# Turning the rank stacks of a four-stage kernel on VectorE and ScalarE instead of TensorE

## Chip, cores and metric

The program runs on one core of a Trainium2 chip. The metric is the device time of one execution in microseconds, 905.26 us as the median of three runs (903.66 to 906.57).

## What is computed

`x` has 64 batches of 64 tokens with 1024 features. Four stages each add something to it, and the stages' indices choose the weights per batch. Cut to what matters:

```python
def reference(x, lang, cond, ad2, ad3, ...):
    # 0: dense W, plus 8 gated low-rank experts (top 2 of 8, rank 16)
    x = x + (x @ W.T + 2.0 * lora(x, gates(x @ Wr.T, lang), A, B))
    # 1: each batch's own 64x64 matrix mixes its 64 tokens
    x = x + einsum('bct,bcd->bdt', x, weights[cond])
    # 2: adapter of the batch, rank 16:  (x B2^T) A2^T
    x = x + einsum('bnr,bor->bno', einsum('bni,bri->bnr', x, B2[ad2]), A2[ad2])
    # 3: dense W3 and bias, plus adapter of the batch, rank 16
    x = x + x @ W3.T + b3 + 2.0 * einsum('btr,bro->bto', einsum('bti,bir->btr', x, A3[ad3]), B3[ad3])
    return x
```

## The kernel before

All dense work is fp32, done as three matmuls of operands rounded to fp32r (high by high, high by low, low by high). ScalarE makes a high part by a rounding copy, VectorE the low part by a subtraction, each waiting for the one before it by a semaphore.

A first phase (to about 340 us) multiplies the stages' matrices into each other. The second phase, 340 us to the end, works through 32 tiles of 128 tokens (two batches of 64 each), in 16 pairs. The code of every engine is unrolled and written by hand: `fore(j, back, fin)` and the rest of `step(j, ...)` for pairs 0 to 14, `fore` and the rest of `last(j)` for pair 15. In pair j the tiles a = 2j and b = 2j + 1 get their dense product (`plain`, and `winograd` for a Strassen-like half), while the two tiles before, a1 = a - 2 and b1 = a - 1 (b2 = a - 3), are finished. The names on the queues (below, `a1` and so on) are these.

The change concerns how a tile is finished. `mixed` writes the mixed tile and, in its first 64 columns, the hidden values of the two adapters (16 ranks for each of two batches and two adapters) to a PSUM bank. Then:

1. `h2_hi` (ScalarE) and `h2_lo` (VectorE) write the high and low parts of adapter 2's ranks to `h2stack`, 128 tokens x 128 columns, in which the columns of the other batch are zero (set once by GpSimd at the start).
2. `h2_rows` (TensorE, line 1486) turns the 128x128 stack into PSUM, `h2T_copy` (ScalarE) rounds it to `h2T`.
3. `ranks2` (TensorE, lines 1503 and 1465) multiplies `h2T` with the adapter's rows `up2`. Its first matmul corrects adapter 3's hidden values and releases `h3_hi`.
4. `h3_hi`, `h3_lo`, `h3_rows` (line 1491), `h3T_copy` and `ranks3` do the same for adapter 3, after which VectorE adds the bias (`add_bias`) and SyncE stores the tile.

These run twice per pair: for a1 wholly inside `fore`, and for b1 with its adapter 2 at the end of `step` and its adapter 3 at the start of the next pair's `fore`. On the ScalarE queue other work stands between: `ud_hi(b)` writes `u2s` and `d3m` from `mdraw`, the next tile's gathered adapter rows, and so waits for their DMA (`ld_md`). SyncE issues that DMA, `load_md(b)`, after `load_up2(a1)`, which waits for `ranks2(b2)`. `gate_exp(a)` gives VectorE the exponential for its chain `gate(a)` (gden to `hg`), behind which stand `hidden_rows(a)`, `h3_lo(a1)` and the low parts of the next operands. `mix_hi(b1)` waits for GpSimd. TensorE's `repeated(b)` (line 1477) needs `vparts` of `hidden_sum(b)`, on VectorE behind `gate(b)`, behind `hgT_lo(a)`, behind `x0_lo(j + 1)`, which follows ScalarE's `x0_hi(j + 1)`.

Of the kernel before, what the change touches and what calls it, by code (L numbers as in the profile page):

```python
# [16 lines left out]
def build(nc, x, stat, mov, a0, wr, wc, u3, u2k, d3k, bias3, lang_ids, ids, out):  # L17
# [137 lines left out]
    with ctx:  # L155
# [116 lines left out]
        h2stack = sb("h2stack", [P, BT, RANK, 2, 2], F32R)  # L272
        h3stack = sb("h3stack", [P, BT, RANK, 2, 2], F32R)
# [26 lines left out]
        ps_hgT, ps_h2T, ps_h3T = ps_s[:, 0:TOKENS], ps_s[:, TOKENS:2 * TOKENS], ps_s[:, 2 * TOKENS:3 * TOKENS]  # L300
# [10 lines left out]
        def plain_bank(t):  # L311

            return ps_d[0] if (t // 2 + t) % 2 == 0 else ps_d[2]

# [5 lines left out]
        def sem(name):  # L320
# [21 lines left out]
        act_h2, act_h2T, act_h3, act_h3T, act_hgT = map(sem, ("act_h2", "act_h2T", "act_h3", "act_h3T", "act_hgT"))  # L342
# [7 lines left out]
        dve_h2, dve_h3, dve_hgT = map(sem, ("dve_h2", "dve_h3", "dve_hgT"))  # L350
# [6 lines left out]
        pe_group, pe_hl, pe_ud, pe_rep, pe_h, pe_mix, pe_h2T, pe_h3, pe_up2, pe_hgT, pe_h3T = map(  # L357
            sem, ("pe_group", "pe_hl", "pe_ud", "pe_rep", "pe_h", "pe_mix", "pe_h2T", "pe_h3", "pe_up2", "pe_hgT", "pe_h3T"))
# [3 lines left out]
        CONSTS = 6  # L362
        SETS = BT + 8
# [14 lines left out]
        def _(sp):  # L378
# [189 lines left out]
            sp.wait_ge(pool_const, CONSTS)  # L568
# [68 lines left out]
        def _(pool):  # L637
# [7 lines left out]
            nc.gpsimd.memset(h2stack[:, :, :, :, :].rearrange("p b r h e -> p (b r h e)").bitcast(F32), 0.0).then_inc(pool_const, 1)  # L645
            nc.gpsimd.memset(h3stack[:, :, :, :, :].rearrange("p b r h e -> p (b r h e)").bitcast(F32), 0.0).then_inc(pool_const, 1)
# [124 lines left out]
        def _(act):  # L771
# [120 lines left out]
            def h2_hi(t):  # L892
                act.wait_ge(pe_h, t + 1)
                for b in range(BT):
                    rows = slice(b * TB, (b + 1) * TB)
                    last = round_to(h2stack[rows, b, :, :, 0], hidden(t, rows, slice(b * RANK, (b + 1) * RANK)))
                last.then_inc(act_h2, 1)

            def h3_hi(t):
                act.wait_ge(pe_h3, t + 1)  # L900
                for b in range(BT):
                    rows = slice(b * TB, (b + 1) * TB)
                    last = nc.scalar.activation(h3stack[rows, b, :, :, 0], hidden(t, rows, slice(BR + b * RANK, BR + (b + 1) * RANK)),
                                                ACT.Copy, scale=SCALE3)
# [59 lines left out]
            def fore(j, back, fin):  # L964
# [10 lines left out]
                if back:  # L975
                    h2_hi(a1)
                gate_exp(a)
                ud_hi(b)
                after_P1(j)
                if back:  # L980
                    h2T_copy(a1)
# [4 lines left out]
            def step(j, back, fin):  # L986
# [10 lines left out]
                if back:  # L997
                    h2_hi(b1)
                ud_hi(a + 2)
# [3 lines left out]
                if back:  # L1003
                    h2T_copy(b1)
# [35 lines left out]
        def _(dve):  # L1040
# [88 lines left out]
            nc.vector.tensor_scalar(rbias[:, :, :], rbias[:, :, :], LANG_BIAS, None, ALU.mult).then_inc(dve_set, 1)  # L1129

# [8 lines left out]
            dve.wait_ge(dve_set, BT + 7)  # L1139
# [72 lines left out]
            def stack_lo(t, rows, b, cols, stacked, scale):  # L1212

                src = out_bank(t, 0)[rows, cols][:, :, None].to_broadcast([TB, RANK, 2])
                return nc.vector.scalar_tensor_tensor(out=stacked[rows, b, :, :, 1], in0=src, scalar=scale,
                                                      in1=stacked[rows, b, :, :, 0].bitcast(F32), op0=ALU.mult,
                                                      op1=ALU.subtract)

# [542 lines left out]
```

## Time and profile before

| | |
|---|---|
| median of three runs | 905.26 us (903.66 to 906.57) |
| profiled execution, its own time | 906.27 us |
| its span | 904.5 us |
| TensorE busy, matmul / weight load | 895.8 us / 795.4 us |
| VectorE, ScalarE, GpSimd busy | 557.5, 345.8, 234.9 us |
| granted TensorE clock | 1.00 throughout |
| two stack transposes on TensorE | 32 of each, mean 271 and 279 ns |
| ScalarE's copies to h2T and h3T | 32 of each, mean 274 and 277 ns |

Durations of matmuls overlap, since they are pipelined; what one costs TensorE is read from start to start. A wait in the profile is put down to what ended it. The profiled time lies 1.8 us above its span, which is what lies around the span, and 1.0 us above the median.

### The profile page before, as it was taken

The page shows a single profiled execution, that of the slowest core. Times are in us where ns is not written, and L with a number is a line of the kernel's source. Part 1 is how long each engine was busy: PE and PEld are TensorE (multiplying, and loading weights), DVE is VectorE, ACT ScalarE, POOL GpSimd, SP SyncE. Part 2 cuts the span into 40 slices and gives each one's busy share as a digit, 9 for nine tenths or more (in the row PEclk, how much of TensorE's full clock was granted, in tenths as well). Part 3 has the DMA queues.
Part 4 walks back from the last instruction along what each step waited for, and adds up shares of the span by engine and source line. Part 5 has one row for each costly group of instructions (what it writes and reads, how often), then busy time and mean ns, then how long its engine had stood idle before and what let it go on. Part 6 is the DMA issues. An engine that isn't in the chain of part 4 may idle for free.

```text
span 904.5 us, 14862 instructions
## 1 busy us (share of the span) xinstructions
PE 895.8 (99%) x4758; PEld 795.4 (88%) x4758; DVE 557.5 (62%) x1421; ACT 345.8 (38%) x800; POOL 234.9 (26%) x379
## 2 busy tenths in 40 slices
PE   9999999999999999999999999999999999999997
PEld 7888888888888888998998998998998999989997
DVE  6655444354357526567667677677676676676675
ACT  5543343333334333333434433434424334334333
POOL 1000010011010003523424433424415325324240
PEclk9999999999999999999999999999999999999999
DMA  7978686999663564666766766766666567666664
GB/s 248 309 252 287 208 252 202 311 338 270 186 190 119 172 211 132 189 179 185 218 181 189 216 188 182 210 194 192 190 197 213 168 189 226 182 174 216 184 199 155
DMA packets 105602, 187.69 MB, mean 208 GB/s; under 512 B 15926, under 2 KB 66870, under 8 KB 105526
## 3 DMA queue, kind: packets, MB, share of 16 engines
q1 hardware_dynamic: 105526, 186.76, 67.7%
q8 instruction: 38, 0.62, 0.3%
q14 instruction: 38, 0.31, 0.1%
HBM read 143.20 MB, written 49.81 MB: 213 GB/s over the span
## 4 chain that ended last, share of the span: by engine, by line
PE 92%; DMA 3%; SPq 2%; issue 1%; POOL 1%; DVE 0%; ACT 0%; DVEq 0%; POOLq 0%
PE ps_o L1407 28%; PE ps_d L1433 17%; PE ps_w L1441 13%; PE ps_d L1441 10%; PE ps_s L1407 9%; PE ps_o L1454 5%; PE ps_d L1448 4%; PE ps_o L1465 2%; DMA mdraw<-t 2%; PE ps_s L1471 1%; SPq L445 1%; PE ps_w L1448 1%; DMA chunk_a_raw<-mov 1%; SPq L473 1%; PE ps_o L1503 1%
## 5 line engine op out<-in xcount | busy, mean ns | idle before, releaser
L1042 DVE TENSOR_TENSOR stat_lo<-stat_raw,stat_hi 128x1024 fp32r<-128x1024 f32 (+1 forms) x127 | 146.3, 1152 | 25.8 <-ACT stat_hi L773 23.5
L773 ACT ACTIVATE stat_hi<-stat_raw 128x1024 fp32r<-128x1024 f32 (+1 forms) x127 | 116.8, 933 | 20.5 <-POOL stat_raw L657 6.3
L1433 PE MATMUL ps_d<-w_hi,stat_hi 128*128 128x512 f32 x256 | 105.0, 410 | 0.0
L1433 PE MATMUL ps_d<-w_lo,stat_hi 128*128 128x512 f32 x256 | 101.1, 395 | 0.0
L1433 PE MATMUL ps_d<-w_hi,stat_lo 128*128 128x512 f32 x256 | 100.8, 394 | 0.0
L1407 PE MATMUL ps_o<-chunk_a_hi,stat_hi 128*128 128x512 f32 x216 | 84.4, 391 | 0.6 <-DVE chunk_a_lo L1042 0.6
L1407 PE MATMUL ps_o<-chunk_a_lo,stat_hi 128*128 128x512 f32 x216 | 84.1, 389 | 0.0
L1407 PE MATMUL ps_o<-chunk_a_hi,stat_lo 128*128 128x512 f32 x216 | 84.0, 389 | 0.0
L682 POOL CAST w_hi<-mdraw 128x512 fp32r<-128x512 f32 x32 | 19.6, 614 | 208.8 <-DMA mdraw<-t 208.8
L657 POOL TENSOR_TENSOR stat_raw<-stat_raw,ident 128x128 f32<-128x128 f32 x40 | 21.8, 546 | 186.3 <-DMA stat_raw<-stat 186.3
L1407 PE MATMUL ps_o<-chunk_b_hi,stat_hi 128*128 128x512 f32 x152 | 59.1, 389 | 0.0
L1407 PE MATMUL ps_o<-chunk_b_hi,stat_lo 128*128 128x512 f32 x152 | 59.1, 389 | 0.0
L1407 PE MATMUL ps_o<-chunk_b_lo,stat_hi 128*128 128x512 f32 x152 | 59.1, 389 | 0.0
L1433 PEld LDWEIGHTS ps_d<-w_lo,stat_hi 128*128 128x128 f32 x256 | 48.1, 188 | 11.4
L1433 PEld LDWEIGHTS ps_d<-w_hi,stat_hi 128*128 128x128 f32 x256 | 48.5, 189 | 9.8 <-DVE udb L1246 0.3
L1433 PEld LDWEIGHTS ps_d<-w_hi,stat_lo 128*128 128x128 f32 x256 | 48.4, 189 | 8.1
L1259 DVE TENSOR_TENSOR outb<-ps_o,bias_row 128x356 f32<-128x356 f32 (+1 forms) x93 | 42.0, 507 | 13.1 <-PE ps_o L1465 12.6
L1407 PEld LDWEIGHTS ps_o<-chunk_a_hi,stat_hi 128*128 128x128 f32 x216 | 40.5, 188 | 9.9 <-DVE chunk_a_lo L1042 1.3
L773 ACT ACTIVATE y_hi<-y_raw 128x356 fp32r<-128x356 f32 x48 | 24.0, 499 | 64.8 <-DVE y_raw L1288 48.8
L1407 PEld LDWEIGHTS ps_o<-chunk_a_lo,stat_hi 128*128 128x128 f32 x216 | 40.6, 188 | 8.5
L1407 PEld LDWEIGHTS ps_o<-chunk_a_hi,stat_lo 128*128 128x128 f32 x216 | 40.6, 188 | 8.2
L718 POOL TENSOR_TENSOR stat_raw<-stat_raw 128x512 f32<-128x512 f32 x32 | 45.3, 1415 | 5.5 <-DMA stat_raw<-x 4.0
(226 smaller groups left out, 2269.7 us busy)
## 6 DMA issues: line engine op xcount, KB each, us to landing
up<-tu SPq DMA_DIRECT2D x124, 256.0 KB, 4.4
stat_raw<-stat SPq DMA_DIRECT2D x59, 512.0 KB, 4.2
mdraw<-t SPq DMA_DIRECT2D x128, 208.0 KB, 2.9
stat_raw<-x SPq DMA_DIRECT2D x32, 512.0 KB, 3.5
out<-outb SPq DMA_DIRECT2D x30, 512.0 KB, 5.4
t<-md_a SPq DMA_DIRECT2D x16, 576.0 KB, 5.8
rows_raw<-x SPq DMA_DIRECT2D x32, 256.0 KB, 3.5
chunk_a_raw<-mov SPq DMA_DIRECT2D x24, 256.0 KB, 5.2
```

The source lines that it names most:

```text
L657: nc.gpsimd.tensor_tensor(out=raw[:, s, :], in0=raw[:, s, :], in1=ident[:, :], op=ALU.add).then_inc(pool_stat, 1)
L682: last = nc.gpsimd.tensor_copy(w[part][:, :, MD_AT:P_AT].rearrange("p k (q r) -> p k q r", r=RANK), rows.rearrange("p q (k r) -> p k q r", ...
L718: nc.gpsimd.tensor_tensor(out=dst, in0=in0, in1=in1, op=op).then_inc(pool_s, 1)
L773: return nc.scalar.activation(dst, src, ACT.Copy)
L1042: return nc.vector.tensor_tensor(out=dst, in0=src, in1=rounded.bitcast(F32), op=ALU.subtract)
L1259: nc.vector.tensor_tensor(out=dst[:, OX[n]], in0=out_bank(turn, n)[:, OK[n]], in1=bias_row[:, OX[n]], op=ALU.add).then_inc(dve_out[n], 1)
L1407: last = nc.tensor.matmul(ps_g[g % BANKS][:, :], st[g % RING][a][:, k, :], mchunk[c % 2][v][:, k, :], start=k == 0 and m == 0, stop=k == K ...
L1433: last = nc.tensor.matmul(plain_bank(t)[:, 0:WCOLS], rows[a][:, k, :], w[c][:, k, :], start=k == 0 and m == 0, stop=k == KB - 1 and m == l ...
L1441: last = nc.tensor.matmul(ps[:, 0:SH], rows[a][:, k, :], weights[c][:, k, :], start=first and k == 0 and m == 0, stop=k == HALF_KB - 1 and ...
L1448: last = nc.tensor.matmul(ps, hgT[t % 2][a][:, :], b03[c][:, cols], start=first and m == 0, stop=m == len(PASSES) - 1, skip_group_check=True)
L1454: last = nc.tensor.matmul(out_bank(turn, n)[:, 0:OW[n]], mix[turn % 2][a][:, :], y[t % 2][c][:, Y[n]], start=first and m == 0, stop=m == l ...
L1465: return nc.tensor.matmul(out_bank(turn, n)[:, OK[n]], stackT[:, :], up[:, OX[n]], start=first, stop=True, skip_group_check=True)
```

## The change

The other batch's columns are no longer kept as zeros in the stack: `h2stack` and `h3stack` are 128 x 64. VectorE turns the whole stack by one operation (`turn_ranks`), which turns each 32x32 square in its place, into one buffer `turned` that all places share. ScalarE then rounds the eight squares to their places in `h2T` or `h3T` by eight operations (`place_squares`); the rest of `h2T` and `h3T` is zeroed once on VectorE. Semaphore `dve_turned` counts the turns and `act_turned` the placings, in one order for both adapters (`h2_place`, `h3_place`), so that a turn waits for the placing before it. `place_squares` also waits until TensorE has read the stack before (`pe_up2` and `pe_h3`, or `pe_out[2]`). `ranks3(b2)` is issued one block of `plain(a)` later (after six blocks, not five), `ranks3(a1)` at the same place but without a transpose halfway. On ScalarE `h2T_copy(a1)` now stands before `gate_exp(a)`, and `h2T_copy(b1)` before `ud_hi(a + 2)`.

```diff
-        h2stack = sb("h2stack", [P, BT, RANK, 2, 2], F32R)
-        h3stack = sb("h3stack", [P, BT, RANK, 2, 2], F32R)
+        h2stack = sb("h2stack", [P, RANK, 2, 2], F32R)
+        h3stack = sb("h3stack", [P, RANK, 2, 2], F32R)
+        turned = sb("turned", [P, 4 * RANK])
...
+        def h2_place(turn):
+            return 2 * turn + (0 if at(turn, TURN_A) else 1)
+        def h3_place(turn):
+            return 2 * turn + (3 if at(turn, TURN_B) else 2)
...
+            def place_squares(rows):
+                for b in range(BT):
+                    for i in range(b * TB, (b + 1) * TB, SQUARE):
+                        for q in range(0, 4 * RANK, SQUARE):
+                            row = b * 4 * RANK + q
+                            last = round_to(rows[row:row + SQUARE, i:i + SQUARE], turned[i:i + SQUARE, q:q + SQUARE])
+                last.then_inc(act_turned, 1)
...
             def h2T_copy(t):
-                act.wait_ge(pe_h2T, t + 1)
-                round_to(h2T[:, :], ps_h2T).then_inc(act_h2T, 1)
+                act.wait_ge(dve_turned, h2_place(t))
+                if not at(t, 0):
+                    act.wait_ge(pe_up2, t)
+                    act.wait_ge(pe_h3, t)
+                place_squares(h2T)
 
             def h3T_copy(t):
-                act.wait_ge(pe_h3T, t + 1)
-                round_to(h3T[:, :], ps_h3T).then_inc(act_h3T, 1)
+                act.wait_ge(dve_turned, h3_place(t))
+                if not at(t, 0):
+                    act.wait_ge(pe_out[2], t)
+                place_squares(h3T)
...
+            def turn_ranks(stacked, place):
+                if place > 1:
+                    dve.wait_ge(act_turned, place - 1)
+                nc.vector.transpose(turned[:, :], stacked[:, :, :, :].rearrange("p r h e -> p (r h e)").bitcast(F32)
+                                    ).then_inc(dve_turned, 1)
...
             def ranks2(t):
-                pe.wait_ge(act_h2T, t + 1)
+                pe.wait_ge(act_turned, h2_place(t))
...
-                plain(a, range(0, 3))
-                if fin:
-                    h3_rows(b2)
-                plain(a, range(3, 5))
+                plain(a, range(0, 6))
                 if fin:
                     ranks3(b2)
-                plain(a, range(5, KB)).then_inc(pe_hl, 1)
+                plain(a, range(6, KB)).then_inc(pe_hl, 1)
...
-                plain(b, range(0, HALF_KB))
+                plain(b, range(KB)).then_inc(pe_hl, 1)
+                if back:
+                    ranks3(a1)
                 pe.wait_ge(dve_udb, a + 1)
-                if back:
-                    h3_rows(a1)
-                plain(b, range(HALF_KB, KB)).then_inc(pe_hl, 1)
-                if back:
-                    ranks3(a1)
                 gated_rows(a)
```

Where instructions move, the queues read as follows. On ScalarE, in `fore` of a pair in the middle, from the high part of the ranks of a1 to its last placing (`part` is the copy of a product out of PSUM), before:

```order
L773 ACTIVATE h2stack<-ps_o 64x32 x2
L887 ACTIVATE gexp<-gdiff 128x1
L773 ACTIVATE u2s<-mdraw 128x2x8x16
L773 ACTIVATE d3m<-mdraw 128x2x8x16
L773 ACTIVATE part<-ps_w 128x356
L773 ACTIVATE h2T<-ps_s 128x128
L773 ACTIVATE mix_hi<-mix_raw 128x128
L903 ACTIVATE h3stack<-ps_o 64x32 x2
L773 ACTIVATE h3T<-ps_s 128x128
```

and now, over the same stretch:

```order
L782 ACTIVATE h2stack<-ps_o 64x32 x2
L782 ACTIVATE u2s<-mdraw 128x2x8x16
L782 ACTIVATE d3m<-mdraw 128x2x8x16
L782 ACTIVATE h2T<-turned 32x32 x8
L896 ACTIVATE gexp<-gdiff 128x1
L782 ACTIVATE part<-ps_w 128x356
L782 ACTIVATE mix_hi<-mix_raw 128x128
L916 ACTIVATE h3stack<-ps_o 64x32 x2
L782 ACTIVATE h3T<-turned 32x32 x8
```

`u2s`, `d3m` (`ud_hi(b)`, behind the DMA of `mdraw`) now come straight after the ranks, then the eight squares to `h2T`, and only then the exponential; the copy out of `part` comes after both.

On VectorE, the end of the program, from the first stack of tile 31 (TURN_A, whose rows come after those of tile 30, TURN_B) to the bias of tile 30 (`y_lo<-ps_w` is `Lb_lo`), before:

```order
L1215 SCALAR_TENSOR_TENSOR h2stack<-ps_o,h2stack 64x32 x2
L1042 TENSOR_TENSOR y_lo<-y_raw,y_hi 128x356
L1215 SCALAR_TENSOR_TENSOR h3stack<-ps_d,h3stack 64x32 x2
L1042 TENSOR_TENSOR y_lo<-ps_w,y_hi 128x356
L1215 SCALAR_TENSOR_TENSOR h3stack<-ps_o,h3stack 64x32 x2
L1259 TENSOR_TENSOR stat_raw<-ps_d,bias_row 128x312
```

and now:

```order
L1244 SCALAR_TENSOR_TENSOR h2stack<-ps_o,h2stack 64x32 x2
L1252 STREAM_TRANSPOSE turned<-h2stack 128x64
L1069 TENSOR_TENSOR y_lo<-y_raw,y_hi 128x356
L1244 SCALAR_TENSOR_TENSOR h3stack<-ps_d,h3stack 64x32 x2
L1252 STREAM_TRANSPOSE turned<-h3stack 128x64
L1069 TENSOR_TENSOR y_lo<-ps_w,y_hi 128x356
L1244 SCALAR_TENSOR_TENSOR h3stack<-ps_o,h3stack 64x32 x2
L1252 STREAM_TRANSPOSE turned<-h3stack 128x64
L1299 TENSOR_TENSOR stat_raw<-ps_d,bias_row 128x312
```

Each stack is followed by its turn, and since a turn waits for the placing before it, the subtraction behind it on VectorE waits too.

## Rows read from the trace of the kernel before

**Rows 1.** Page, busy time of each engine over the span.
```profile
PE 895.8 (99%) x4758; PEld 795.4 (88%) x4758; DVE 557.5 (62%) x1421; ACT 345.8 (38%) x800; POOL 234.9 (26%) x379
```

**Rows 2.** Waits over the whole span: us in total, times, longest.
```profile
ACT u2s L773 <- DMA mdraw<-t: 46.8, 28, 3.5
...
PEld ps_s L1491 <- issue: 5.2, 10, 1.1
...
PE ps_s L1491 <- DVE h3stack L1215: 1.4, 3, 0.7
```

**Rows 3.** PE timeline, pair 7: start us, duration us, instruction.
```profile
588.64 0.33 PE L1441 MATMUL ps_w<-B_lo,stat_hi 128*128 128x356 f32 x1
588.80 0.27 PE L1486 MATMUL ps_s<-ident,h2stack 128*128 128x128 f32 x1
588.83 0.41 PE L1441 MATMUL ps_d<-B_hi,stat_hi 128*128 128x356 f32 x1
589.08 0.33 PE L1441 MATMUL ps_d<-B_hi,stat_lo 128*128 128x356 f32 x1
...
590.88 0.32 PE L1503 MATMUL ps_o<-up,h2T 128*128 128x344 f32 x1
...
594.04 0.40 PE L1433 MATMUL ps_d<-w_lo,stat_hi 128*128 128x512 f32 x1
594.53 0.30 PE L1491 MATMUL ps_s<-ident,h3stack 128*128 128x128 f32 x1
...
597.47 0.64 PE L1465 MATMUL ps_o<-up,h3T 128*128 128x312 f32 x3
```

**Rows 4.** Tile ps_s, transposes of h2stack: count, ns min/median/max, first and last start.
```profile
L1486 PE MATMUL ps_s<-ident,h2stack x32: 270/270/274, 379.5 to 894.9; 128*128 128x128 f32 x32
```

**Rows 5.** ACT timeline of the same pair.
```profile
586.07 0.40 ACT L773 ACTIVATE h2stack<-ps_o 64x32 fp32r<-64x32 f32 x2 [0.78 <-PE ps_o L1454]
...
588.81 0.42 ACT L773 ACTIVATE u2s<-mdraw 128x256 fp32r<-128x256 f32 x1 [0.33 <-DMA mdraw<-t]
589.14 0.40 ACT L773 ACTIVATE d3m<-mdraw 128x256 fp32r<-128x256 f32 x1
...
593.36 0.31 ACT L773 ACTIVATE mix_hi<-mix_raw 128x128 fp32r<-128x128 f32 x1 [3.17 <-POOL mix_raw L706]
593.58 0.38 ACT L903 ACTIVATE h3stack<-ps_o 64x32 fp32r<-64x32 f32 x2
```

**Rows 6.** ACT groups by shape: busy us, mean ns, idle before.
```profile
L773 ACT ACTIVATE stat_hi<-stat_raw 128x1024 fp32r<-128x1024 f32 x91 | 96.0, 1055 | 10.7 <-DMA stat_raw<-x 5.3 <-POOL stat_raw L657 5.3
...
L773 ACT ACTIVATE y_hi<-y_raw 128x356 fp32r<-128x356 f32 x48 | 24.0, 499 | 64.8 <-DVE y_raw L1288 48.8 <-DVE y_raw L1273 15.9
...
L773 ACT ACTIVATE h2stack<-ps_o 64x32 fp32r<-64x32 f32 x62 | 12.0, 193 | 15.4 <-PE ps_o L1454 15.0
...
L773 ACT ACTIVATE mix_hi<-mix_raw 128x128 fp32r<-128x128 f32 x32 | 9.9, 310 | 63.5 <-POOL mix_raw L706 63.5
```

**Rows 7.** ACT and PE timeline, the two pairs with the widest and narrowest margin.
```profile
658.58 0.40 ACT L773 ACTIVATE d3m<-mdraw 128x256 fp32r<-128x256 f32 x1
...
660.65 0.32 PE L1503 MATMUL ps_o<-up,h2T 128*128 128x344 f32 x1
...
834.94 0.40 ACT L773 ACTIVATE d3m<-mdraw 128x256 fp32r<-128x256 f32 x1
...
836.05 0.43 PE L1503 MATMUL ps_o<-up,h2T 128*128 128x344 f32 x1
```

**Rows 8.** DVE and PE timeline, pair 7: last vparts and its reader.
```profile
602.45 0.18 DVE L1239 TENSOR_TENSOR vparts<-vsum,vparts 64x32 fp32r<-64x32 f32 x1
...
603.49 0.18 PE L1477 MATMUL ps_s<-vparts,repeat 128*128 128x32 f32 x1
```

**Rows 9.** ACT and PE timeline, end of the program.
```profile
898.88 0.28 ACT L773 ACTIVATE h3T<-ps_s 128x128 fp32r<-128x128 f32 x1 [1.22 <-PE ps_s L1491]
...
899.21 0.73 PE L1465 MATMUL ps_o<-up,h3T 128*128 128x312 f32 x3
```

More of the change, by code:

```diff
@@ L893, in h2_hi @@
                 act.wait_ge(pe_h, t + 1)
+                if not at(t, 0):
+                    act.wait_ge(dve_turned, h2_place(t - 1))
                 for b in range(BT):
                     rows = slice(b * TB, (b + 1) * TB)
-                    last = round_to(h2stack[rows, b, :, :, 0], hidden(t, rows, slice(b * RANK, (b + 1) * RANK)))
+                    last = round_to(h2stack[rows, :, :, 0], hidden(t, rows, slice(b * RANK, (b + 1) * RANK)))
                 last.then_inc(act_h2, 1)
@@ L976, in fore @@
                     h2_hi(a1)
+                ud_hi(b)
+                if back:
+                    h2T_copy(a1)
                 gate_exp(a)
-                ud_hi(b)
                 after_P1(j)
                 if back:
-                    h2T_copy(a1)
                     mix_hi(b1)
@@ L998, in step @@
                     h2_hi(b1)
+                    h2T_copy(b1)
                 ud_hi(a + 2)
@@ L1129, in _ @@
             nc.vector.tensor_scalar(rbias[:, :, :], rbias[:, :, :], LANG_BIAS, None, ALU.mult).then_inc(dve_set, 1)
+            for rows in (h2T, h3T):
+                nc.vector.tensor_copy(rows[:, :], mixraw[:, :]).then_inc(dve_set, 1)
             for first in (0, 2 * BR):
@@ L1221, in h2_lo @@
                 for b in range(BT):
-                    last = stack_lo(t, slice(b * TB, (b + 1) * TB), b, slice(b * RANK, (b + 1) * RANK), h2stack, 1.0)
+                    last = stack_lo(t, slice(b * TB, (b + 1) * TB), slice(b * RANK, (b + 1) * RANK), h2stack, 1.0)
                 last.then_inc(dve_h2, 1)
+                dve.wait_ge(dve_h2, t + 1)
+                turn_ranks(h2stack, h2_place(t))
             def h3_lo(t):
@@ L1227, in h3_lo @@
                 for b in range(BT):
[L1228 removed]
+                    last = stack_lo(t, slice(b * TB, (b + 1) * TB), slice(BR + b * RANK, BR + (b + 1) * RANK), h3stack, SCALE3)
                 last.then_inc(dve_h3, 1)
+                dve.wait_ge(dve_h3, t + 1)
+                turn_ranks(h3stack, h3_place(t))
             def hidden_sum(t):
@@ L1482, in gated_rows @@
                 nc.tensor.transpose(ps_hgT, hg[:, :, :].rearrange("p e r -> p (e r)"), ident[:, :]).then_inc(pe_hgT, 1)
-            def h2_rows(t):
-                pe.wait_ge(dve_h2, t + 1)
-                nc.tensor.transpose(ps_h2T, h2stack[:, :, :, :, :].rearrange("p b r h e -> p (b r h e)").bitcast(F32),
-                                    ident[:, :]).then_inc(pe_h2T, 1)
-            def h3_rows(t):
-                pe.wait_ge(dve_h3, t + 1)
-                nc.tensor.transpose(ps_h3T, h3stack[:, :, :, :, :].rearrange("p b r h e -> p (b r h e)").bitcast(F32),
-                                    ident[:, :]).then_inc(pe_h3T, 1)
             def hidden_ranks(turn, t):
```

61 lines of the change are left out of this document (24 added, 37 removed).

## Prediction, made before the changed kernel ran

> **What bounds the kernel now.** I began with the page: TensorE is busy 895.8 of 904.5 us, ScalarE only 38%, VectorE 62% [rows 1]. The view of the waits says the same from the other side: TensorE waits for nobody in the second phase but in front of the transpose of `h3stack`, 1.4 us for VectorE and 5.2 us of its weight loads without a named releaser [rows 2]. So every slot taken off TensorE is worth its length, and every wait put on it costs its length; what the other engines spend counts only through such waits. The timeline of one pair in the middle (pair 7, about 34.8 us, as the 13 from 2 to 14 are) then shows how far ahead of TensorE the other queues are where the change touches them.
>
> **What is removed.** A transpose is shown as 270 ns [rows 4], but that is its latency. From start to start: 588.64 to 588.80 is 0.16 for a product of 356 columns; with the transpose between, 588.80 to 589.08 is 0.28 [rows 3]. So a transpose takes 0.115 of TensorE, and 64 of them 7.4 us, 55 in pairs 1 to 14 (6.3 us), 9 in the last. The waits before `h3_rows(a1)` go too: 594.04 to 594.53 is 0.49 where a 512-column product is else followed after 0.24 (twelve and the transpose fill 594.53 to 597.47) [rows 3]. Weights are loaded about a slot ahead, so of the 6.6 us of these waits [rows 2] in 13 places I take 13 x 0.25 as covered and 3.2 us as lost. Together 9.5 us saved in pairs 1 to 14.
>
> **What is added: the price of a placing.** Eight ScalarE operations of 32x32 from SBUF. From SBUF, 128 columns take 310 ns and 356 take 499 [rows 6], 0.83 ns a column, so 32 take 230. How closely do they follow one another? `u2s` takes 0.42 and `d3m` starts 0.33 after it; `mix_hi` takes 0.31 and `h3stack` starts 0.22 after it [rows 5]: an overlap of 0.09. But the two operations of `h2stack`, of 193 ns [rows 6], take 0.40 together [rows 5], no overlap. Length isn't what differs, I think, but place: that pair goes from partitions 0 to 63 to partitions 64 to 127, while the overlapping ones start at the same partition. In `place_squares` each square goes to another group of partitions than the one before, so I take 0.24 apiece, 1.91 for eight. The bound from below is the overlap, 0.14 apiece, 1.2 for eight. The Trainium skill (VectorE: DVE Perf Modes, section on two Vector instructions with no wait between them) has a rule for this: an instruction whose start quadrant differs from that of the last access is held until all before it have finished. It states it for VectorE; rows 5 look as if ScalarE does the same. The same page (section on the TRN2 errata) warns that many small tiles pay the fixed latency each time, which speaks against eight squares in place of one copy.
>
> The turn on VectorE, 128x64 from SBUF, has no row. The nearest are a 64x32 operation, 0.18 [rows 8], and ScalarE's 128x128 copy at 0.31; I take 0.25, with 0.15 and 0.6 as ends. It sits in chains with slack, except in (c) and (d).
>
> **(b) ranks2(a1).** Its operand now comes last out of: DMA of `mdraw`, `u2s`, `d3m`, eight squares. In pair 7 `d3m` ends at 589.54 (589.14 + 0.40), held by the DMA [rows 5], as in 28 cases of `ud_hi` [rows 2], and before, one copy followed and `ranks2` started at 590.88 [rows 3], a margin of 1.34. The DMA's issue hangs on `ranks2(b2)` through SyncE's queue, so it doesn't move relative to TensorE. Now the squares end 1.91 - 0.09 after `d3m`, and 0.05 later TensorE goes: 1.87. TensorE itself arrives 0.23 earlier, two transposes being gone. The wait is 2.10 less the margin: 0.76 here. The margin was read in all 13 pairs 2 to 14: from 0.71 (834.94 + 0.40 to 836.05) to 1.67 (658.58 + 0.40 to 660.65) [rows 7], mean 1.08. That makes 13 x 1.02 = 13.2 us, and the first pair, whose landing is late too, 1.3 more: **14.5 us of new waits**.
>
> **(c) Behind it.** The exponential comes after the squares, so VectorE's gate chain starts up to 3 us later. Counting through the queues of pair 7 from the start R of `ranks2(a1)`, with the chain of `gate(b)` as the model for an undisturbed gate: exponential at R, `hg` at R + 1.8, `udb` R + 3.1, `h3_lo` done R + 3.6, turned R + 4.0, placed R + 6.0; TensorE reaches `ranks3(a1)` at R + 6.17 (597.47 - 590.88 less the 0.42 of transpose and wait [rows 3]). Just in time. Then `x0_hi` (1.05 for 1024 columns [rows 6]) and `x0_lo` (about 1.2) end at R + 8.3, 0.5 later than before, and with them all up to `vparts(b)`, which was ready at 602.63 for a reader at 603.49 [rows 8], but with TensorE 0.42 later than it now is: it lacks 0.1. I take 0.13 x 14 = 1.8 us. `ranks3(b2)` gets its stack 1.3 later, is itself 0.6 later (a block more, a transpose less) and had 0.9 in hand: no wait. `h2T_copy(b1)` runs where ScalarE otherwise waits for the DMA of `mdraw` [rows 2]: nothing. The start loses two memsets on GpSimd and gains two copies on VectorE under the first phase's products: nothing.
>
> **(d) The last pair.** Here the chains lie behind one another and TensorE has little else. By the same prices, with the one buffer `turned` in series, TensorE's lag behind its old times is 0.3 us at `ranks3(a1)`, 0.8 at `ranks2(b1)`, 1.8 at `ranks3(b1)`, 2.3 at tile 30's `ranks2`, 2.6 at tile 31's, 3.3 at tile 30's `ranks3`, 5.8 at tile 31's. The last step is the largest: before, a copy of 0.28 at 898.88 let the last matmuls start at 899.21 [rows 9]; now the stack of tile 31 is written after the squares of tile 30 and `Lb`, then turned, then placed by 1.9 us. The bias of tile 30 is out of the way by then (0.3): **+5.5 us**, the nine transposes counted.
>
> **The sum.** -9.5 + 14.5 + 1.8 + 5.5 = +12.3 us. The profiled execution took 906.27 us (its span and 1.8 around it) and would take 918.6; the median of the runs lies 1.0 lower, so 917.6, and I say 918. With placings of 1.8 to 2.0 us, and the small waits of (c) between none and double, 910 to 925.
>
> **Rivals.**
> 1. *The squares overlap* (placing 1.2 us). Then the waits of (b) are 1.40 less the margin, 5.0 us with the first pair, those of (c) vanish, the last pair costs about 2: -9.5 + 5.0 + 2 = -2.5, **902.8 us**. For it speak the overlaps of rows 5, against it the pair of `h2stack` there. It decides below about 0.16 us per square. By the Trainium skill (ScalarE: Activation LUTs, section What ACT_TABLE_LOAD costs) an ACTIVATE with immediate scale takes 186 ns + 0.833 ns a column and back-to-back ones overlap by about 93 ns; by that, eight would take 1.05 us and the time would be about 901, an estimate from that page. Chance 0.22.
> 2. *The turn is slow or is hindered by GpSimd* (0.6 us instead of 0.25). It stands three times in each pair's tight chains: `ranks3(a1)` then waits 0.2 and (c) 0.35 more, 14 x 0.45 = 6 us, and 1.5 in the last pair: **925 us**. For it speaks only that no row shows such an operation; against it, that every row of VectorE with up to 64 columns lies near 0.2. Chance 0.10.
> 3. *The waits and savings cancel*, if the squares take about 0.18 each or the `mdraw` rows land a microsecond sooner, since the DMA is less crowded when TensorE stands: -9.5 + 9 + 1 = about 0, **906 us**. Chance 0.06.
>
> The forecast has 0.62. 0.3% is 2.7 us, about what a measurement of this kernel can tell from no change. Rival 1 lies about that bound and goes mostly to faster: faster 0.18, same 0.09, slower 0.73. The range reaches to rival 1 and rival 2: 901 to 925.
>
> **What would show it.** Right: TensorE's waits name ScalarE's `h2T` in front of `ranks2` in nearly all 14 pairs, some 1 us each, and `h2T` groups of eight last 1.9 us; ScalarE's busy time grows by about 100 us; the gate's `gden` waits for `gexp` in every pair; the last matmuls start 5 to 6 us later relative to the last pair's start. Wrong: squares that start 0.14 apart; TensorE without waits at `ranks2`, with a span about 5 us below mine for each 0.03 us a square is cheaper; or waits in front of `ranks3(a1)`, which would mean a slow turn.

## The result, and the profile after

The changed kernel takes 932.0 us (median of six runs, 926.1 to 941.9); the kernel before, on the same chip, 905.2 us. The ratio is 1.029, interval 1.025 to 1.033 (it leaves out the slowest run, 941.9, which lies over 1.5% above the fastest): 27 us slower, where the forecast was 13. The profiled execution took 926.12 us, 19.9 more than the one before; its span is 924.2 us, its mean granted clock 0.995. The other runs have clocks from 0.995 down to 0.986, and their times rise as the clock falls. Before, it was 1.00.

The page, busy time of each engine:

```profile
PE 900.4 (97%) x4694; PEld 792.2 (86%) x4694; DVE 549.3 (59%) x1487; ACT 444.0 (48%) x1248; POOL 234.8 (25%) x377
```

Against [rows 1], ScalarE has 98 us more. TensorE has 64 instructions fewer and is busy 4.6 us longer, which is the first oddity. The squares, from the page's costliest groups (busy us, mean ns, idle before):

```profile
L782 ACT ACTIVATE h3T<-turned 32x32 fp32r<-32x32 f32 x256 | 57.9, 226 | 30.7 <-DVE turned L1252 28.1
...
L782 ACT ACTIVATE h2T<-turned 32x32 fp32r<-32x32 f32 x256 | 57.9, 226 | 13.0 <-DVE turned L1252 10.3
```

The waits over the span (us in total, times, longest), to be held against [rows 2]:

```profile
DVE gden L1205 <- ACT gexp L896: 42.8, 17, 4.5
...
ACT u2s L782 <- DMA mdraw<-t: 41.3, 17, 4.1
...
PEld ps_o L1533 <- ACT h2T L782: 16.0, 15, 2.5
...
PE ps_o L1533 <- ACT h2T L782: 11.6, 14, 2.2
...
PE ps_o L1505 <- ACT h3T L782: 3.0, 2, 1.7
...
PEld ps_s L1522 <- DVE udb L1286: 2.4, 11, 0.2
...
PEld ps_s L1517 <- DVE vparts L1279: 1.7, 8, 0.3
```

L1533 is the first product of `ranks2`: the forecast's wait stands there, in 14 of 15 pairs. Something stands there that wasn't forecast. The timeline of pair 6, the one with the longest wait (start us, duration us):

```profile
554.88 0.89 SPq L468 DMA_DIRECT2D mdraw<-t  x2
...
562.41 0.42 ACT L782 ACTIVATE u2s<-mdraw 128x256 fp32r<-128x256 f32 x1 [4.09 <-DMA mdraw<-t]
...
563.04 1.88 ACT L782 ACTIVATE h2T<-turned 32x32 fp32r<-32x32 f32 x8
...
564.97 0.19 PEld L1533 LDWEIGHTS ps_o<-up,h2T 128*128 128x128 f32 x1 [2.52 <-ACT h2T L782]
564.98 0.43 PE L1533 MATMUL ps_o<-up,h2T 128*128 128x344 f32 x1 [2.23 <-ACT h2T L782]
...
565.92 0.40 PE L1473 MATMUL ps_d<-w_hi,stat_lo 128*128 128x512 f32 x1
...
566.15 0.40 PE L1473 MATMUL ps_d<-w_lo,stat_hi 128*128 128x512 f32 x1
...
567.16 0.63 PE L1473 MATMUL ps_d<-w_lo,stat_hi 128*128 128x512 f32 x1
...
567.58 0.63 PE L1473 MATMUL ps_d<-w_hi,stat_hi 128*128 128x512 f32 x1
```

The rows land 7.5 us after their issue (554.88, and `u2s` starts at 562.41), where it is 5.5 to 6.3 in the 14 pairs of the kernel before; two roundings and eight squares follow; TensorE stands from 562.75 (the end of its last product) to 564.98. Then, from about 566.5, the same products of 512 columns start 0.42 us apart and not 0.23. The stretches of that time (PE, PEld, DVE, ACT and POOL busy, granted clock, DMA share, GB/s) say why:

```profile
563.00:565.00 2.00, 0.02 (x1) 0.03 (x1) 0.00 (x0) 1.89 (x10) 2.00 (x5) 1.00 0.65 157
565.00:566.00 1.00, 1.00 (x6) 0.95 (x7) 0.64 (x4) 0.97 (x5) 0.63 (x2) 1.00 0.57 229
566.00:567.00 1.00, 1.00 (x5) 0.80 (x4) 0.90 (x5) 0.12 (x1) 0.01 (x1) 0.75 0.04 16
567.00:568.00 1.00, 1.00 (x3) 0.73 (x3) 0.96 (x4) 0.00 (x0) 0.00 (x0) 0.50 0.70 246
568.00:569.00 1.00, 1.00 (x4) 0.80 (x3) 0.95 (x5) 0.23 (x2) 0.00 (x0) 0.50 0.87 238
569.00:570.00 1.00, 1.00 (x4) 0.81 (x3) 1.00 (x3) 0.95 (x5) 0.00 (x0) 0.55 0.16 41
570.00:571.00 1.00, 1.00 (x6) 0.79 (x6) 0.70 (x2) 0.95 (x4) 0.00 (x0) 1.00 0.00 0
```

TensorE ran at 0.50 of its clock, the lower of its levels (1.2 GHz), for 3.4 us, 1.5 us after it had gone to work again. The same follows the wait of pair 1, the second longest (2.0 us in this view), and no other in this profile before the end of the program. Each period costs 1.7 us (half of 3.4), and since a slow product counts as busy, TensorE's busy time grows.

Further small waits sit around the gate's transpose. From pair 11's timeline:

```profile
757.55 0.25 DVE L1286 SCALAR_TENSOR_TENSOR udb<-ps_s,is_lo,vsign 128x32 fp32r<-128x32 f32 x1
757.60 0.33 PE L1481 MATMUL ps_d<-T_lo,stat_hi 128*128 128x356 f32 x1
757.85 0.14 PEld L1522 LDWEIGHTS ps_s<-ident,hg 128*128 128x128 f32 x1 [0.22 <-DVE udb L1286]
757.86 0.33 PE L1522 MATMUL ps_s<-ident,hg 128*128 128x128 f32 x1
758.17 0.41 PE L1494 MATMUL ps_o<-y_hi,mix_hi 128*128 128x376 f32 x1
```

The transpose comes 0.1 late (0.26 after the product ahead of it, where 0.16 is normal), and the product behind it starts 0.31 after it; in the kernel before that step is 0.05 on average. A wait of 0.1 costs 0.3.

The end, of tile 31's stack:

```profile
917.12 0.24 DVE L1252 STREAM_TRANSPOSE turned<-h3stack 128x64 f32<-128x64 f32 x1
...
917.40 1.90 ACT L782 ACTIVATE h3T<-turned 32x32 fp32r<-32x32 f32 x8 [0.89 <-DVE turned L1252]
...
919.35 0.74 PE L1505 MATMUL ps_o<-up,h3T 128*128 128x312 f32 x3 [1.75 <-ACT h3T L782]
```

It answers to [rows 9]. From `ranks2` of pair 15 to these last matmuls it takes 28.4 us before and 33.5 now: 5.1 more.

**Where the time is.** Profiled run against profiled run, +19.7 us of span: +1.9 up to pair 1's `ranks2`, +12.5 from there to pair 14's, +0.6 to pair 15's, +5.1 in the last part, -0.4 behind it. I took every start-to-start step of TensorE from the records and compared them kind by kind. A wait is from here on such a step less the usual 0.16, so it is 0.16 longer than in the views (pair 6: 2.39 for 2.23). For pairs 1 to 14 this gives: waits at `ranks2(a1)` +12.6 (13.2 now, 0.43 to 2.39 in 13 pairs and none in pair 7; the kernel before waited 0.6 in pair 1), the products that restart behind them +1.2, two periods at half clock +3.4, the steps at `repeated` and `gated_rows` +4.7, one wait of 1.5 at `ranks3(b2)` in pair 7, transposes and their waits -9.4. Together +14.0. Up to pair 14's `ranks2` 14.4 is there, and of that 0.5 is lost in the first phase already, by 122 us.

### The profile page after: what moved, and what is told of

Same layout as the page of the kernel before. It is cut to its first block, busy times and chain, and to the rows that moved or that the text cites. A ratio compares the mean times of both kernels' runs of the same rounds, so it can differ in the third digit from the quotient of the medians.

```text
span 924.2 us, 15418 instructions
## 1 busy us (share of the span) xinstructions
PE 900.4 (97%) x4694; PEld 792.2 (86%) x4694; DVE 549.3 (59%) x1487; ACT 444.0 (48%) x1248; POOL 234.8 (25%) x377
## 4 chain that ended last, share of the span: by engine, by line
PE 74%; SPq 8%; DMA 8%; ACT 4%; issue 4%; DVE 2%; POOL 0%; DVEq 0%; ACTq 0%; POOLq 0%
PE ps_o L1447 26%; PE ps_d L1473 11%; PE ps_w L1481 10%; PE ps_s L1447 9%; DMA mdraw<-t 7%; PE ps_d L1481 6%; PE ps_d L1488 4%; SPq L455 3%; PE ps_o L1494 3%; ACT h2T L782 3%; SPq L483 2%; PE ps_o L1505 2%; SPq L468 2%; PE ps_o L1533 1%; SPq L470 1%
## 5 line engine op out<-in xcount | busy, mean ns | idle before, releaser
L1069 DVE TENSOR_TENSOR stat_lo<-stat_raw,stat_hi 128x1024 fp32r<-128x1024 f32 (+1 forms) x127 | 137.0, 1079 | 38.5 <-ACT stat_hi L782 36.2
L691 POOL CAST w_hi<-mdraw 128x512 fp32r<-128x512 f32 x32 | 19.7, 615 | 208.6 <-DMA mdraw<-t 208.6
L782 ACT ACTIVATE h3T<-turned 32x32 fp32r<-32x32 f32 x256 | 57.9, 226 | 30.7 <-DVE turned L1252 28.1
L782 ACT ACTIVATE h2T<-turned 32x32 fp32r<-32x32 f32 x256 | 57.9, 226 | 13.0 <-DVE turned L1252 10.3
```

The lines of the kernel that those rows point to most:

```text
L691: last = nc.gpsimd.tensor_copy(w[part][:, :, MD_AT:P_AT].rearrange("p k (q r) -> p k q r", r=RANK), rows.rearrange("p q (k r) -> p k q r", ...
L782: return nc.scalar.activation(dst, src, ACT.Copy)
L1069: return nc.vector.tensor_tensor(out=dst, in0=src, in1=rounded.bitcast(F32), op=ALU.subtract)
```

## Experiments

Theory: TensorE's waits at `ranks2(a1)` hang on the landing of the `mdraw` rows and on the squares behind it; the longest of them cost a second time, through the clock. Rivals: the squares cost wherever they stand; the clock falls for another reason; the gate that comes late is the main loss. All ratios are to runs of the kernel before on the same chip, whose medians were 905.4 to 906.0 us.

**The earlier rows, e2.**

```
-                if back:
-                    load_up2(a1)
                 if not at(j, 0):
                     choose(b)
                     load_md(b)
+                if back:
+                    load_up2(a1)
```

(and likewise in the last pair)

> SyncE issues the load of the second tile's rows ahead of the load of the first tile's rank rows, in every pair; nothing else differs from the changed kernel. Theory A (the wait at the first rank products is set by the landing of these rows, 5.3 to 7.6 us after their issue, since the rounding of them stands ahead of the squares on ScalarE): the landing moves 1 to 2 us earlier, the waits shrink by as much, from 13.6 us to some 2 us over 14 pairs, no half clock is seen, and the time is 912 to 917 us. Rival B (the issue waits for a buffer that comes free no earlier, or the transfers share the same queues so that the landing stays): the waits stay as they are, 926 to 932 us. Rival C: the rank rows now land too late for the same products: a wait of TensorE for that load, 930 us or more.

907.8 us (ratio 1.0023, 1.0008 to 1.0038): 24 of the 27 us are gone, by an exchange of two loads in a queue. Timeline of pair 9:

```profile
650.13 0.88 SPq L468 DMA_DIRECT2D mdraw<-t  x2
...
656.03 0.42 ACT L782 ACTIVATE u2s<-mdraw 128x256 fp32r<-128x256 f32 x1 [0.36 <-DMA mdraw<-t]
...
656.66 1.89 ACT L782 ACTIVATE h2T<-turned 32x32 fp32r<-32x32 f32 x8
...
658.57 0.20 ACT L896 ACTIVATE gexp<-gdiff 128x1 f32<-128x1 f32 x1
...
659.93 0.32 PE L1533 MATMUL ps_o<-up,h2T 128*128 128x344 f32 x1
```

The squares last 1.89 us as they did, but end 1.4 us ahead of the product. No wait at `ranks2` is left over 0.15 us in pairs 1 to 14, and no half clock before the end (0.998). Theory A: the landing was what `ranks2` waited for. The time is 4 us under the range that I gave. Between the profiled spans lie 17.8 us and between the medians 24.2, so part of this gain is in what the slower runs of the changed kernel have above the profiled one.

**The squares first, e1.** ScalarE's list: squares, exponential, `ud_hi`, where the change has `ud_hi`, squares, exponential.

> ScalarE's list in the first half of a pair is put in another order: the squares of the first tile stand ahead of the exponential of the gate and ahead of the u2s rounding, so that they no longer wait for the rows that a transfer brings. Theory A (the changed kernel's time comes from TensorE's waits at the first rank products, of 0.43 to 2.39 us a pair and 13.6 us over 14 pairs, and from the half-clock periods behind the two longest of them, 3.4 us in the profiled run): these waits and both periods go, and so does what follows on them. The removed transposes' gain of 9.4 us stays, and the last pair keeps its 4.7 us: some 901 us, with the clock at 1.00 up to the last pair. Rival B (the squares themselves slow the kernel wherever they stand, since ScalarE then does everything behind them 1.9 us later: the u2s rounding and with it the hidden product, the gate): the wait moves to another product, 915 us or more. Rival C (the clock falls for another reason than the waits): half-clock periods stay in the trace though the waits are gone.

914.3 us (1.011, 1.008 to 1.014). The waits at `ranks2` and the half clock went; the 901 did not come. The rows are still late here, and now `ud_hi` stands behind them and the squares, so `vparts` and `udb` are late in their turn: in the waits, `ps_s` L1517 for `vparts` has 3.5 us in 11 places and L1522 for `udb` 3.0 in 13, and the steps there add up to 7.4 us more than before over 13 pairs. My expectation left out what stands behind the squares; Rival B has a part in it.

**The gate first, e3 and e7.** The exponential and `ud_hi` ahead of the squares, once with the late rows and once with the early ones.

```
-                ud_hi(b)
-                if back:
-                    h2T_copy(a1)
                 gate_exp(a)
+                ud_hi(b)
+                if back:
+                    h2T_copy(a1)
```

> Only the exponential of the gate and the u2s rounding change places with the squares in the first half of a pair: exponential, rounding, squares. The wait for the rows stays ahead of the squares, so the waits at the first rank products stay (13.6 us) and the half-clock periods with them. What can move is the other part: in the changed kernel the exponential stands behind the squares, some 4.5 us later against the rest than before, and VectorE's chain behind it makes the gate's transpose and the products next to it late, 0.1 to 0.3 us at three places, 4.7 us over 14 pairs. Theory A: these 4.7 us go, 926 to 928 us. Rival B: they hang on the h3 rows' late squares and not on the gate: no change, 932 us.

> Both orders together: SyncE issues the load of the second tile's rows ahead of the rank rows (which took the first rank products' wait away, 907.8 us), and ScalarE takes the gate's exponential and the u2s rounding ahead of the squares (which took the small waits around the gate's transpose away, 4 us over 14 pairs). Theory A: the two costs are apart and add: no wait at the first rank products, none around the gate, the removed transposes' 9.4 us stay, the last pair costs its 4.7 us: 901 to 904 us, no slower than the kernel before. Rival B (the exponential ahead pushes the squares 0.6 us later, past the margin that the earlier rows gave): part of the waits comes back, 906 to 910 us.

e3: 922.0 us (918.7 to 928.2; 1.020, 1.014 to 1.025). The steps around the gate are back at those of the kernel before (their sum is 0.6 us under it, from 4.7 above), while the waits at `ranks2` (17.0 us, 3.8 more than in the changed kernel) and two half-clock periods stayed. So the gate's place was worth its 4.7 us. The median is 10 us lower, and 4 us under what Theory A said, where the profiled spans differ by 3.7; no trace shows the rest. But e7 took 915.4 us, 7.6 worse than e2. Its timeline, pair 10:

```profile
696.90 0.61 POOL L691 CAST w_hi<-mdraw 128x512 fp32r<-128x512 f32 x1 [1.59 <-DMA mdraw<-t]
...
698.73 0.20 ACT L896 ACTIVATE gexp<-gdiff 128x1 f32<-128x1 f32 x1 [2.13 <-DVE gdiff L1199]
...
699.46 1.89 ACT L782 ACTIVATE h2T<-turned 32x32 fp32r<-32x32 f32 x8
...
701.39 0.42 PE L1533 MATMUL ps_o<-up,h2T 128*128 128x344 f32 x1 [0.36 <-ACT h2T L782]
```

The rows are there at 696.9, but ScalarE stands for 2.1 us at the exponential, which waits for VectorE, with the squares queued behind it. `ranks2` waits in every pair again, 0.46 us at least. The two gains are not independent, as I had assumed. It is Rival B's mechanism, and 5 us more than the most that Rival B gave: the exponential's own wait for VectorE was in neither sum.

**The price of a square, e4, e9 and e10.** e4:

```
-                for b in range(BT):
-                    for i in range(b * TB, (b + 1) * TB, SQUARE):
-                        for q in range(0, 4 * RANK, SQUARE):
-                            row = b * 4 * RANK + q
-                            last = round_to(rows[row:row + SQUARE, i:i + SQUARE], turned[i:i + SQUARE, q:q + SQUARE])
+                for q in range(0, 4 * RANK, SQUARE):
+                    for i in range(0, TOKENS, SQUARE):
+                        last = round_to(rows[q:q + SQUARE, i:i + SQUARE], turned[q:q + SQUARE, q:q + SQUARE])
```

> The same sixteen squares a tile and the same 32 x 32 elements each, but read from and written to the same partitions: four from partitions 0 to 31 into partitions 0 to 31, then four from 32 to 63 into 32 to 63. The rank products multiply something else by it; nothing else differs. Theory A (two roundings on ScalarE overlap by 0.09 us only while the range of partitions stays the same, as my prediction took it): six of the seven steps in a group shrink from 0.240 to 0.15 us, a group lasts 1.35 us and not 1.89, each first rank product starts 0.5 us earlier, and with fewer half-clock periods the time is 918 to 924 us. Rival B (the step of 0.24 us is that of a square of 32 columns and 32 partitions, whatever it touches): a group lasts 1.89 us and the time is the changed kernel's, 926 to 934 us.

Its timeline, and the time 908.0 us (1.0029, 1.0008 to 1.005):

```profile
399.79 0.25 DVE L1250 STREAM_TRANSPOSE turned<-h2stack 128x64 f32<-128x64 f32 x1
400.07 1.19 ACT L782 ACTIVATE h2T<-turned 32x32 fp32r<-32x32 f32 x8 [0.74 <-DVE turned L1250]
```

The products multiply something else by this edit, so the run tells of time alone. A group lasts 1.19 us and not 1.89. Inside it squares start 0.120 us apart, 0.224 at the one step that changes partitions; each takes 0.213, so they overlap by 0.093. The first `ranks2` waits fall from 13.2 to 6.8 us, the half clock is gone from the profiled run, the steps around the gate are 1.4 us above those before and not 4.7, and the last part takes 30.1 us. Theory A, and by 10 us more than I had it. The ten runs fall into two groups: six of 903.9 to 908.7 us with clocks of 0.998 and 0.999, four of 910.6 to 912.1 with 0.994 to 0.996, so longer waits and half clock still come in some. By the Trainium skill (ScalarE: Activation LUTs, section What ACT_TABLE_LOAD costs) back-to-back ones overlap by about 93 ns: the trace agrees where the partitions stay, and shows none of it where they change.

e9 asks which of the two ranges counts: squares with the same destination stand one behind the other, their sources differ.

```
-                    for i in range(b * TB, (b + 1) * TB, SQUARE):
-                        for q in range(0, 4 * RANK, SQUARE):
+                    for q in range(0, 4 * RANK, SQUARE):
+                        for i in range(b * TB, (b + 1) * TB, SQUARE)[::1 if q == 0 else -1]:
```

> The changed kernel with its eight squares in another sequence and nothing else: the two that go to the same partitions stand one behind the other (the source's partitions change between them), so that four of the seven steps in a group keep the destination's partitions. The run with all squares in place had steps of 0.120 us where both ranges stayed and 0.224 us where both changed. Theory A (it is the destination's range that decides): a group lasts 0.22 + 4 x 0.12 + 3 x 0.24 = 1.4 us and not 1.89, the first rank products' waits shrink by 0.5 us each, and the time is 914 to 922 us. Rival B (a change of either range keeps two roundings apart): all steps stay at 0.24 us, 926 to 934 us.

931.3 us, all steps 0.237 to 0.241, the group 1.90: Rival B. In the change's own sequence it is the destination that changes at every step, and the source at three of seven; here the source changes at five and the destination at three. Either keeps two squares apart. That the partitions have to be the same, and not the elements (in e4 four squares read the same source), `u2s` and `d3m` show, which differ in their elements alone and overlap by 0.09 [rows 5]. With the early rows the new sequence does nothing either:

> The new sequence of the squares together with the earlier load of the second tile's rows. If the sequence shortens a group to 1.4 us, what was left in the version with the earlier rows, small waits around the gate's transpose of some 0.4 us a pair, shrinks too, and the last pair has 8 groups that are 0.45 us shorter, three or four of them on its path: 903 to 906 us. If the sequence changes nothing: 907.8 us again.

907.9 us (1.0027, 1.0016 to 1.0038).

**The clock, e5 and e6.** e5 puts six idle products of 356 columns ahead of `ranks2(a1)`. e6 makes the squares later:

```
+                if at(t % 2, 0):
+                    for n in range(4):
+                        round_to(spare[n * SQUARE:(n + 1) * SQUARE, 0:SQUARE], turned[n * SQUARE:(n + 1) * SQUARE, 0:SQUARE])
                 place_squares(h2T)
```

> Six products of 356 columns (some 1.0 us) that do no work are put ahead of the first rank products of every pair, where TensorE waits; they add to columns of the output tile, which this run leaves changed. Theory A (a wait of some 2.2 us and more drops the clock to half for 3.4 us): the waits of 0.43 to 2.39 us become 0 to 1.4 us, the clock stays at 1.00 up to the last pair, and though TensorE has more to do the time falls or stays: the products cost only where the wait was under 1.0 us, some 3.5 us in all, and the half-clock periods (3.4 us in the profiled run, 5 to 6 us in the median run by its mean clock) go: 928 to 931 us. Rival B (the clock falls for another reason): half-clock periods stay and the time is the changed kernel's and 3.5 us: 935 us.

> Four more squares, into a tensor that nobody reads, stand on ScalarE ahead of the first tile's squares in every pair, so that each wait of TensorE at the first rank products grows by 0.95 us, from 0.43 to 2.39 us to some 1.4 to 3.3 us. Without a cost of its own a longer wait adds 14 x 0.95 = 13.3 us: Rival B, 945 us. Theory A (a wait of over some 2.1 us is followed by 3.4 us at half clock, which costs 1.7 us on top): it happens in at least eight of the fourteen pairs and not in one or two, the mean clock falls to 0.98 or under, and the time is 955 to 965 us.

e5: 930.5 us (927.9 to 931.7), clocks 0.995 to 0.998 where the changed kernel has 0.986 to 0.995. One half-clock period is left in the profiled run, behind a wait of 2.04 us that remained behind the idle products in pair 13. Filled waits bring most of the clock back, though TensorE has 14 us more to do; the time is Theory A's.

e6: 945.8 us (942.5 to 958.2), clocks 0.989 down to 0.978, the slowest run with the lowest clock. The wait at `ranks2` in its profile, and the granted clock around pair 6:

```profile
PE ps_o L1537 <- ACT h2T L783: 29.8, 15, 3.9
```

```profile
572.00:573.00 1.00, 0.00 (x0) 0.00 (x0) 0.00 (x0) 0.95 (x5) 0.42 (x1) 1.00 0.48 188
573.00:574.00 1.00, 0.63 (x5) 0.63 (x5) 0.32 (x2) 0.94 (x5) 0.45 (x1) 1.00 0.03 12
574.00:575.00 1.00, 1.00 (x5) 0.86 (x4) 0.86 (x5) 0.51 (x4) 0.21 (x1) 0.64 0.02 8
575.00:576.00 1.00, 1.00 (x3) 0.72 (x3) 0.97 (x4) 0.00 (x0) 0.00 (x0) 0.50 0.55 106
```

Eight of the fourteen waits have half clock at their end, against two in the changed kernel: the count of Theory A. The time is at Rival B's 945 all the same in the median, and the clock fell less than I said (0.983 in the profiled run of 949.2 us, 0.988 in the median one). Between the profiled runs it can be counted: up to pair 15's `ranks2` e6 takes 22.9 us more than the changed kernel. The waits at `ranks2` grew by 17.5, six more periods at half clock stand for 10.2, the steps around the gate are 3.0 less and the wait at `ranks3(b2)`, 1.5, is gone: 23.2. With 1.7 us for each period the sum comes out, and a TensorE that comes later finds small waits behind filled. Why the median runs have fewer periods is open.

Over all traces that show waits here (changed kernel, e3 to e9), a wait of at most 1.77 us was never followed by half clock, one of 3.3 to 4.1 us always (four), and of those from 1.85 to 2.7 us eleven of fifteen. In one of the eleven (e6, pair 14, 2.38 us) the half clock began 0.2 us before TensorE went on. What decides between these fifteen is open.

**Was it slow before? e12.** The kernel before with the earlier rows.

> The kernel before with SyncE's earlier load of the second tile's rows, nothing else. Theory A (before, the rows' landing was hidden by 0.9 us on average ahead of the first rank products and only the changed kernel waits on it): the time stays within 1 us of 905.3 us. Rival B (the load was late before too, and the gain of the version with the earlier rows is not the changed kernel's own): some 3 us less, 902 us, which are the waits of 3.2 us that TensorE has there for the transposes' stacks.

904.2 us (0.9989, 0.9980 to 0.9997): 1.2 us less, a tenth of a per cent. The late landing was nearly free before; it is the change that made it the bound.

**The last pair, e8 and e11.** VectorE places four of each eight squares of the last two turns, four copies of 0.17 us that start 0.19 apart; once on e7, once on e10.

```
+            def place_half(rows, place):
+                dve.wait_ge(dve_turned, place)
+                for b in range(BT // 2, BT):
...
+                            last = nc.vector.tensor_copy(rows[row:row + SQUARE, i:i + SQUARE], turned[i:i + SQUARE, q:q + SQUARE])
+                last.then_inc(dve_placed, 1)
```

> As the version with both orders, and in the last pair alone the squares of the last two turns are shared: ScalarE places four of each eight, VectorE the other four. Theory A (the last pair's 4.7 us come from groups of eight squares that stand on the path to the end, 1.9 us each, two of them with nothing of TensorE's beside them): each shared group ends some 0.8 us earlier, the last wait shrinks from 1.9 to 1.1 us, and the time is 1.5 to 3 us under that of the version with both orders. Rival B (VectorE's own list is full there, and its four squares of some 0.2 us each make its additions behind them late): the time stays or rises by up to 1 us.

> The same, and in the last pair alone VectorE places four of each of the last turns' eight squares. Sharing took 2.5 us off the version with both orders. With shorter groups it is worth less: 1 to 2 us under the run without it, 902 to 904 us, no slower than the kernel before. Rival B: VectorE's four squares cost it 0.75 us a group there and its additions become late: no gain.

912.9 us (1.0072) against 915.4, and 907.0 (1.0018, 1.0009 to 1.0027) against 907.9. The last wait shrinks from 1.91 to 0.96 us in both, and from `ranks2` of pair 15 on 1.4 and 1.7 us are saved, but another wait there grows from 0.3 to 1.3; it ends with VectorE's `outb`, and VectorE's list is longer.

**The best places for the exponential, e13 to e16.** All have the early rows. e13: four squares, exponential, four squares. e14: squares, exponential, `ud_hi`. e15 and e16 are these two with the shared last pair.

> The version with the earlier rows (907.8 us), and the gate's exponential stands between the fourth and the fifth square of the first tile's group, 0.95 us earlier than behind them. Theory A (the small waits around the gate's transpose, some 6 us over 14 pairs, come from the exponential's delay of 1.2 us behind its place in the kernel before): they go for the most part, the first rank products keep a margin of over 0.5 us, and the time is 902 to 904 us. Rival B (the waits come from the squares' load on ScalarE wherever the exponential stands): 907 to 909 us. Rival C (the exponential itself waits for the gate's differences there, and holds the last four squares up past the margin): waits at the first rank products of 0.3 to 0.5 us again, 910 us or more.

> The version with the earlier rows, and ScalarE takes the whole group of squares first, then the exponential, then the u2s rounding, for which the rows lie there by then. The exponential comes 0.7 to 0.8 us earlier than in the version with the earlier rows, the u2s rounding 1.5 to 2 us later. Theory A: the gate's small waits shrink to a third and the later rounding is still in time for the second tile's products: 903 to 905 us. Rival B (the later rounding makes VectorE's and GpSimd's work on the rows late, as in the run with the squares first and the late rows, 914.3 us): 908 us or more.

> As the version with the exponential between the squares, and in the last pair VectorE places four of each of the last turns' eight squares, which took 0.9 to 2.5 us off two other versions: 1 to 2 us under the run without it. Theory A for both parts gives 900.5 to 902.5 us, faster than the kernel before; if only the last pair's part holds, 906 us.

> As the version with the squares ahead of the exponential, and the shared squares in the last pair: 1 to 2 us under the run without it, 901.5 to 904 us by Theory A for both parts, 906 us or more if the later u2s rounding costs what Rival B says.

906.4 us (1.0013, 0.9998 to 1.0028), 907.6 (1.0017), 906.5 (1.0003, 0.9992 to 1.0014) and 906.8 (1.0006, 0.9997 to 1.0015), beside 905.6 for the kernel before. The best of them equal it; none beats it. e13 and e14 lie between their Theory A and Rival B. The shared last pair gave nothing on e13 and 0.8 us on e14, where 1 to 2 were expected. In e13's profile pairs 1 to 15 take 484.3 us, where they take 488.6 before and 501.8 in the changed kernel, and e2's take 486.3: some 4 of the 9.9 us of transposes and waits are kept. The rest goes in small waits, chiefly at `repeated` and the gate's transpose (3.3 us above before over 13 pairs; 5.0 in e2), and the last part gives 5.1 back (33.5 us against 28.4).

## Why the prediction was wrong

Direction and place were right, the size was not: 918 said with 901 to 925, 932.0 measured. By its steps, in the profiled runs:

- **What is removed**, 9.5 us: 9.4 found. The start-to-start price of a transpose, 0.115 and not the 270 ns that its row shows, holds. (By its own rows 13 x 0.25 is what the waits cost, not what was covered; the sum stays.)
- **The price of a placing**, 1.91 us: 1.89 found, the turn 0.245 for 0.25, 98 us on ScalarE for 100. The reason, a change of partitions, is shown by e4 and e9.
- **(b), the wait at `ranks2(a1)`**, 14.5 us: 13.2 found, and 12.6 more than before, since pair 1 waited 0.6 there already. The arithmetic held, 2.10 less the margin, but it took the margins of one profile as they were. The rows land 4.8 to 7.5 us after their issue now, 5.5 to 6.3 before, at a mean of 5.9 for 6.0; with no margin left every late landing reaches TensorE whole, and an early one gives nothing back.
- **The step that failed: a wait was priced at its length.** The sum has no term for what follows a wait. Half-clock periods cost 3.4 us in the profiled run and restarts behind `ranks2` 1.2, the largest part of the 7.6 us by which its growth of 19.9 exceeds the 12.3 forecast. The median lies another 5.9 us higher. The two runs in its middle, 931.5 and 932.5 us, have clocks of 0.994 and 0.991 against 0.995; a period takes 0.0018 off the clock, so they would have half a period and two more, 1 and 4 us. That is inferred from the clocks, since those runs left no trace, and the other half of the 5.9 us is open.
- **(c), the gate**, 1.8 us: 4.7 found, the second part. "It lacks 0.1" at `repeated(b)` was near (0.03 to 0.19 late in eight of 13 pairs), but the same delay comes through at the gate's transpose, and a wait of 0.1 there costs 0.3 by the product behind it. "`ranks3(b2)`: no wait" fell in pair 7, by 1.5 us: the next tile's rows landed 7.2 us after their issue, GpSimd made `mix_raw` behind them, and `h3stack` stands behind its rounding on ScalarE. "The start: nothing" was 0.5 us.
- **(d), the last pair**, 5.5 us: 5.1 found.
- **Rivals.** Rival 1, squares that overlap, is e4: it gives 908.0 and not 902.8, the group's 1.19 us as assumed; the waits left are 6.8 us for the 5.0 taken, the gate's steps 1.4 for none. Rival 2 fell with the turn's 0.245 us. Rival 3's hope, that rows land earlier while TensorE stands, fell too: their mean went from 6.0 to 5.9 us.
- **The range.** Its upper end held the bounds of each known price, but nothing for run-to-run spread, though a kernel whose waits hang on landings must have one: 926 to 942 us against 904 to 907.

## What to carry to other kernels

When TensorE waits where it never did, price the wait twice: by its length, and by what comes behind it. Look in the clock's row behind waits of about 2 us and more.

Before work is moved to an idle engine, ask what that engine waits for ahead of it: here a load that had been hidden by 1 us became the bound, and exchanging two loads in a queue (e2) returned 24 of 27 us. Where a DMA's landing is in a margin, one profile doesn't give it: the same load took 4.8 to 7.5 us from pair to pair.

On ScalarE, keep the partition range the same from one small operation to the next; a change of source or destination doubled the step (0.120 to 0.24 us).

## What the runs showed of the hardware

- Two ScalarE operations of 32x32 from SBUF start 0.120 us apart with the same partitions and 0.237 to 0.241 with other source or destination partitions. The Trainium skill (VectorE: DVE Perf Modes, section on two Vector instructions with no wait between them) states such a rule for VectorE, for what is read and what is written; e4 and e9 show both on ScalarE.
- VectorE copies the same squares in 0.17 us, 0.19 apart, and turns 128x64 in 0.245.
- The granted clock fell to 0.50 for 3.4 us at waits of 1.9 to 4 us, mostly 0.6 to 1.6 us after TensorE had gone back to work (in e6 once 0.2 after and once 0.2 before), and products of 512 columns then start 0.42 us apart. A wait of 2.41 us was once not followed by it (e3), one of 1.88 once was (e6).
- One and the same load (`load_md(b)`) landed 5.5 to 6.3 us after its issue in the kernel before and 4.8 to 7.5 in the changed one. The waits at `ranks2` don't explain the spread: e1 has none and its loads took 5.3 to 7.5. Why is open.
